# Mamba stage: the last token tile of states one to ten scaled by B on VectorE instead of GpSimd

## The chip, the cores and the metric

One core of one Trainium2 chip runs a whole two-layer decoder as one program. The metric is the device time of one execution in microseconds. The kernel before took 4200.27 us (median of 3 runs, 4198.12 to 4200.87).

Engine names: PE is TensorE (PEld its weight loads), DVE is VectorE, ACT is ScalarE, POOL is GpSimd, SP is SyncE, which issues the DMAs.

## The reference, cut to what matters

The decoder has six sublayers, each followed by a residual and a layer norm. The change lies in the fourth, a Mamba block over 32 sequences of 256 tokens, with 512 inner channels and 16 states:

```
dt    = softplus(log_dt @ W_dt.T + b_dt)          # tokens x 512
A_bar = exp(dt[..., None] * A)                    # tokens x 512 x 16
Bu    = dt[..., None] * B_coef[:, :, None, :] * xc[..., None]
h     = A_bar * h + Bu                            # along the tokens, per channel and state
y     = sum over the 16 states of h * C_coef
```

For one state s this means: u = dt * xc (tokens x 512 channels) is multiplied by one number per token, B[:, s]; a recurrence runs along the tokens for each channel; its result is multiplied by C[:, s] and summed over the states.

## The kernel before

The stage works on 16 groups of two sequences (512 tokens). Inside a group it goes through the 16 states s, and inside a state through 4 chunks c of 128 channels. I write (s, c) for such a step, and the names below are functions inside `mamba`.

For each state the work is:

- `scale_b` (L2003 on, ACT) multiplies u by B[:, s]. u lies with tokens on the partitions, in 4 token tiles of 128 x 512 (`uT`), so that B is one number per partition (`b_t`). In states 1 to 10 ACT does only three of the four tiles, and `scale_tile` on POOL (L2125, operation on L2130) does the fourth. The product is `bu`, double buffered by state.
- `turn_state` (PE, L1825) turns chunk c of `bu` with four 128x128 transposes into one of two PSUM buffers `pbu`. For c = 0 it waits for ACT's tiles and for the fourth (`tile_ready`). It also waits for the scan two steps before, whose PSUM buffer it takes.
- `decay` (ACT, L2021) makes exp(dt * A).
- `scan` (DVE, L2227) runs the recurrence on chunk c: data from `a` in SBUF and `pbu` in PSUM, result `h`.
- `times_c` (POOL, L2123) multiplies `h` by C, both read from SBUF, into `ch`.
- `sum_state` (PE, L1834) adds the turned chunk to the output `py` in PSUM, five steps later.

Between these steps each engine does, at fixed places written out by hand, the work that prepares the next group and finishes the one before. All engines work through their lists in order. Those that matter here:

- DVE: `gate` (L2235) around (0, 3) and (1, 0); `convolve` (L2197) in states 2 to 5, one operation between scans 0 and 1, two between scans 1 and 2; `finish` (L2255) before scans (7, 0), (7, 1), (10, 2), (10, 3), which waits for `rstd_of` on POOL (L2145, L2146); `one_plus` (L2207, 128x1024 f32 from SBUF to SBUF) right before scans (9, 1) and (10, 1); `lost_part` (L2213) and `take_lost` (L2221), which read two SBUF tensors each.
- PE: `project_x` (L1764) after (1, 3) to (4, 3), from the second on waiting for the convolution before; `add_skip` (L1841), `parameters` (L1787) and `spread_l` (L1794) in states 6 and 7; `project_out` (L1870, L1872) in states 4, 5, 8 and 9.
- POOL: `scale_tile(s + 1)` directly behind `times_c(s, 0)`, for s = 0 to 9; `rstd_of` behind (6, 2) and (10, 0).

Group 0 has no group before it, the last group prepares none. The groups in between run in a hardware loop whose body holds two groups.

Of the kernel before, what the change touches and what calls it, by code (L numbers as in the profile page):

```python
# [10 lines left out]
ALU = mybir.AluOpType  # L11
# [3 lines left out]
P = 128  # L15
# [1562 lines left out]
def mamba(nc, x_in, x_out, ct_dram, g_d, win_d, wout_d, conv_d, wx_d, dtp_d, alog_d, ident_d):  # L1578
# [5 lines left out]
    DI = wout_d.shape[0]  # L1584
    IC = DI // P
# [3 lines left out]
    TT = GB * T  # L1589
    GS = GB * S  # L1590
    K = N * IC
    xf_in = x_in.rearrange("(g b) (t p) d -> g p (b t) d", b=GB, p=P)
    xf_out = x_out.rearrange("(g b) (t p) d -> g p (b t) d", b=GB, p=P)
    with Stage(nc, "ma") as st:
# [28 lines left out]
        b_t = sb("b_t", [P, 2, TT, N])  # L1623
# [4 lines left out]
        uT = sb("uT", [P, 2, TT, DI])  # L1628
# [36 lines left out]
                 (wx_cols[:, :, :], wx_d.rearrange("(c p) f -> p c f", p=P)),  # L1665
                 (conv[:, :, :], conv_d), (dtp[:, :, :], dtp_d), (A[:, :, :], alog_d)]

        def on_pool(s):
            return 1 <= s <= 10

        def groups(eng, group, link=None, turns=NG // 2 - 1):
# [73 lines left out]
        def _(pe):  # L1745
# [71 lines left out]
            def turn_state(g, s, c):  # L1817

                if c == 0:
                    pe.wait_ge(bu_ready, N * g + (s + 1))  # L1820
                    if on_pool(s):
                        pe.wait_ge(tile_ready, 10 * g + s)
                pe.wait_ge(scanned, K * g + (IC * s + c + 7))
                for t in range(TT):
                    last = pe.transpose(pbu[c % 2][:, t * P:(t + 1) * P], bu[:, s % 2, t, c * P:(c + 1) * P], ident[:, :])  # L1825
                last.then_inc(bu_turned, 1)
# [110 lines left out]
        def _(act):  # L1937
# [67 lines left out]
            def scale_b(g, par, s):  # L2005

                if s == 0:
                    act.wait_ge(uT_copied, IC * g + IC)
                    act.wait_ge(b_copied, g + 1)
                act.wait_ge(bu_turned, K * g + (IC * s + 4))  # L2010
                for t in range(TT - 1 if on_pool(s) else TT):
                    last = act.activation(bu[:, s % 2, t, :], uT[:, par, t, :], ACT.Copy, scale=b_t[:, par, t, s:s + 1])  # L2012
                last.then_inc(bu_ready, 1)

# [87 lines left out]
        @block.gpsimd  # L2102
        def _(pool):
            link = Chain(pool, pool_chain, 2 * (2 + IC + 2))

            def rms_of(n):
                pool.wait_ge(ssq_ready, TT * n + TT)
                link(pool.tensor_tensor(ms[:, :], ssq[:, :], eps6[:, :], ALU.add))
                link.mark(pool.tensor_tensor(rms[:, :], ms[:, :], minus_half[:, :], ALU.pow))

            def rms_diagonal(n):
                link.wait()
                if not (type(n) is int and n == 0):
                    pool.wait_ge(xT_made, 2 * n)
                pool.tensor_tensor(rdiag[:, :, :], ident[:, :].unsqueeze(1).broadcast_to([P, TT, P]),
                                   rms[:, :].unsqueeze(2).broadcast_to([P, TT, P]), ALU.mult).then_inc(rdiag_ready, 1)

            def times_c(g, s, c):
                pool.wait_ge(scanned, K * g + (IC * s + c + 9))
                if c == 0:  # L2120
                    pool.wait_ge(c_loaded[s % 4], (4 * 16) * g + 16 * (s // 4 + 1))
                pool.wait_ge(summed, K * g + (IC * s + c + 1))
                pool.tensor_tensor(ch[:, s % 2, c], h[:, c], crep[:, s % 4, :], ALU.mult).then_inc(multiplied, 1)  # L2123

            def scale_tile(g, par, s):  # L2125

                if s == 1:
                    pool.wait_ge(uT_copied, IC * g + IC)
                pool.wait_ge(bu_turned, K * g + (IC * s + 4))
                pool.tensor_tensor(bu[:, s % 2, TT - 1, :], uT[:, par, TT - 1, :],  # L2130
                                   b_t[:, par, TT - 1, s:s + 1].broadcast_to([P, DI]), ALU.mult).then_inc(tile_ready, 1)

            def step_input(n, par, c, k):

                if k == 0:
                    pool.wait_ge(rest_ready, IC * n + (c + 1))
                    link(pool.tensor_tensor(dt[:, par, c, :], dt[:, par, c, :], ln1[:, c, :], ALU.add))
                    pool.sem_inc(dt_ready, 1)
                else:
                    pool.tensor_tensor(u[:, c, :], dt[:, par, c, :], xc[:, par, c, :], ALU.mult).then_inc(u_ready, 1)  # L2140

            def rstd_of(g, half):
                k = slice(2 * half, 2 * half + 2)
                pool.wait_ge(var_ready, 2 * g + (half + 1))
                link(pool.tensor_tensor(veps[:, k], mv[:, k, 1], eps5[:, k], ALU.add))  # L2145
                pool.tensor_tensor(rstd[:, k], veps[:, k], minus_half[:, k], ALU.pow).then_inc(rstd_ready, 1)  # L2146

            def group(g, par, first, last):
                n, prep = g + 1, not last
                ahead = not (type(g) is int and g + 2 >= NG)  # L2150
                for s in range(N):
                    for c in range(IC):
                        times_c(g, s, c)
                        if c == 0 and on_pool(s + 1):
                            scale_tile(g, par, s + 1)
                        if prep and (s, c) in ((11, 1), (12, 0), (12, 3), (13, 2)):
                            step_input(n, 1 - par, (4 * s + c - 44) // 3, 0)
                        if prep and (s, c) in ((11, 2), (12, 1), (13, 0), (13, 3)):
                            step_input(n, 1 - par, (4 * s + c - 45) // 3, 1)
                        if (s, c) in ((6, 2), (10, 0)) and not first:  # L2160
                            rstd_of(g - 1, 0 if s == 6 else 1)
                        if s == 5 and c == 2 and ahead:
                            rms_of(g + 2)
                        if s == 7 and c == 2 and ahead:
                            rms_diagonal(g + 2)

            pool.memset(eps6[:, :], 1e-6 * D)
            pool.memset(eps5[:, :], LN_EPS)
            pool.memset(ones[:, :], 1.0)
            link(pool.memset(minus_half[:, :], -0.5))  # L2170
            pool.wait_ge(w_loaded, 16 * len(loads))
            pool.sem_inc(multiplied, IC)
            pool.sem_inc(summed, 2 * IC)
            rms_of(0)
            rms_diagonal(0)
            for c in range(IC):
                for k in range(2):
                    step_input(0, 0, c, k)
            rms_of(1)
            rms_diagonal(1)  # L2180
            groups(pool, group, link, turns=NG // 2 - 2)
            for half in range(2):
                rstd_of(NG - 1, half)

        @block.vector
        def _(dve):
# [36 lines left out]
            def scan(g, s, c):  # L2223
# [3 lines left out]
                dve.tensor_tensor_scan(out=h[:, c, :], data0=a[:, s % 2, c, :], data1=pbu[c % 2][:, :],  # L2227
                                       initial=0.0, op0=ALU.mult, op1=ALU.add).then_inc(scanned, 1)

            def gate(g, par, t):  # L2230

                if t == 0:
                    dve.wait_ge(sz_ready, g + 1)
                    dve.wait_ge(summed, K * g + (K + 8))
                dve.tensor_tensor(gT[:, t, :], py[:, t, :], sz[:, par, t, :], ALU.mult).then_inc(gated, 1)  # L2235
# [24 lines left out]
            def group(g, par, first, last):  # L2260
                n, prep, ahead = g + 1, not last, not (type(g) is int and g + 2 >= NG)
                for s in range(N):
                    for c in range(IC):
                        if not first and (s, c) in ((0, 3), (1, 0)):
                            for t in (2 * s, 2 * s + 1):
                                gate(g - 1, 1 - par, t)
                        if 2 <= s < 2 + IC and c in (1, 2) and prep:
                            for k in ((1,), (2, 3))[c - 1]:
                                convolve(n, 1 - par, s - 2, k)
                        if not first and (s, c) in ((6, 0), (6, 1), (9, 2), (9, 3)):  # L2270
                            y_stats(g - 1, c)
                        if not first and (s, c) in ((6, 2), (10, 0)):
                            y_var(g - 1, 0 if s == 6 else 1)
                        if not first and (s, c) in ((7, 0), (7, 1), (10, 2), (10, 3)):
                            finish(g - 1, c)
                        if prep and (s, c) in ((9, 1), (10, 1)):
                            one_plus(n, s - 9)
                        if prep and (s, c) in ((11, 0), (12, 0)):
                            lost_part(n, s - 11)
                        if prep and (s, c) in ((11, 1), (11, 3), (12, 2), (13, 0)):  # L2280
                            take_lost(n, {(11, 1): 0, (11, 3): 1, (12, 2): 2, (13, 0): 3}[s, c])
                        scan(g, s, c)

            for p in range(2):
                dve.memset(a[:, p], 0.0)
# [469 lines left out]
```

## Time and profile before

| | |
|---|---|
| median of 3 runs | 4200.27 us |
| profiled execution | 4201.03 us, its span 4199.2 us |
| Mamba stage, first to last scan | 1342 to 3246 us from the span's start |
| mean granted TensorE clock | 0.941 of full speed |
| DVE / POOL / ACT / PE busy, whole span | 3128.6 / 2717.5 / 2909.9 / 3510.9 us |

A row of a timeline gives start, duration, engine, line, operation, written and read tensors, count, and in brackets the idle time of the engine before it with what ended it. Rows of one operation that follow each other directly are merged into one with a count, and its duration is then that of all. An operation's recorded duration holds time in which it was started and held up.

### The profile page before, as it was taken

The page shows a single profiled execution, that of the slowest core. Times are in us where ns is not written, and L with a number is a line of the kernel's source. Part 1 is how long each engine was busy: PE and PEld are TensorE (multiplying, and loading weights), DVE is VectorE, ACT ScalarE, POOL GpSimd, SP SyncE. Part 2 cuts the span into 40 slices and gives each one's busy share as a digit, 9 for nine tenths or more (in the row PEclk, how much of TensorE's full clock was granted, in tenths as well). Part 3 has the DMA queues.
Part 4 walks back from the last instruction along what each step waited for, and adds up shares of the span by engine and source line. Part 5 has one row for each costly group of instructions (what it writes and reads, how often), then busy time and mean ns, then how long its engine had stood idle before and what let it go on. Part 6 is the DMA issues. An engine that isn't in the chain of part 4 may idle for free. (4 is left out here: it accounts for less than half of the span.)

```text
span 4199.2 us, 73811 instructions
## 1 busy us (share of the span) xinstructions
PE 3510.9 (84%) x22848; PEld 2545.8 (61%) x22848; DVE 3128.6 (75%) x5241; ACT 2909.9 (69%) x5201; POOL 2717.5 (65%) x2890
## 2 busy tenths in 40 slices
PE   8996999989844888888888888888888799994666
PEld 5664666775422667666666666666667577762333
DVE  5666888844684788778878787787777477776988
ACT  2224888833565888887878888787887377774766
POOL 1224666610483998898989889898988355552555
PEclk9998999979867999999999999999999899997999
DMA  2111111151121111111111111111111111112111
GB/s 60 55 53 45 42 42 43 39 111 36 28 71 50 45 48 53 45 52 49 52 50 47 52 43 54 51 50 50 47 47 43 41 41 40 40 34 70 50 46 35
DMA packets 199386, 204.57 MB, mean 49 GB/s; under 512 B 45768, under 2 KB 164104, under 8 KB 199064
## 3 DMA queue, kind: packets, MB, share of 16 engines
q1 hardware_dynamic: 199064, 200.65, 16.3%
q8 instruction: 156, 2.56, 0.2%
q14 instruction: 166, 1.36, 0.1%
HBM read 149.18 MB, written 51.41 MB: 48 GB/s over the span
## 5 line engine op out<-in xcount | busy, mean ns | idle before, releaser
L2227 DVE TENSOR_TENSOR_SCAN ma_h<-ma_a,ma_pbu 128x512 f32<-128x512 f32 x1024 | 1223.2, 1211 | 344.9 <-PE ma_pbu L1825 180.2
L2123 POOL TENSOR_TENSOR ma_ch<-ma_h,ma_crep 128x512 f32<-128x512 f32 x1024 | 1338.1, 1324 | 201.3 <-DVE ma_h L2227 185.0
L1825 PE MATMUL ma_pbu<-ma_ident,ma_bu 128*128 128x128 f32 x4096 | 659.4, 285 | 175.9 <-DVE ma_h L2227 129.6
L1825 PEld LDWEIGHTS ma_pbu<-ma_ident,ma_bu 128*128 128x128 f32 x4096 | 484.5, 145 | 420.6 <-DVE ma_h L2227 279.6
L1834 PE MATMUL ma_py<-ma_ident,ma_ch 128*128 128x128 f32 x4096 | 637.9, 280 | 42.2 <-POOL ma_ch L2123 30.3
L2021 ACT ACTIVATE ma_a<-ma_dt,ma_A 128x510 f32<-128x510 f32 x1024 | 652.9, 717 | 1.4 <-issue 1.4
L2012 ACT ACTIVATE ma_bu<-ma_uT,ma_b_t 128x512 f32<-128x512 f32 x864 | 556.7, 718 | 11.8 <-PE ma_pbu L1825 10.1
L1834 PEld LDWEIGHTS ma_py<-ma_ident,ma_ch 128*128 128x128 f32 x4096 | 492.0, 145 | 70.2 <-POOL ma_ch L2123 64.4
L856 POOL TENSOR_TENSOR xa_prob<-xa_e,xa_rec_head 128x616 f32<-128x616 f32 x256 | 307.3, 1217 | 310.7 <-DVE xa_rec_head L945 309.9
L936 DVE TENSOR_REDUCE xa_top<-xa_pS 128x8 f32<-128x616 f32 x256 | 202.9, 793 | 149.6 <-PE xa_pS L625 142.2
L765 ACT ACTIVATE xa_eT<-xa_pE 77x512 f32<-77x512 f32 x512 | 276.7, 594 | 49.3 <-PE xa_pE L637 47.5
L637 PE MATMUL xa_pE<-xa_ident,xa_prob 128*77 128x128 f32 x2048 | 277.0, 279 | 4.8 <-POOL xa_prob L856 4.5
L637 PEld LDWEIGHTS xa_pE<-xa_ident,xa_prob 128*77 128x77 f32 x2048 | 228.2, 149 | 60.1 <-issue 32.9
L944 DVE TENSOR_REDUCE xa_esum<-xa_e 128x8 f32<-128x616 f32 x256 | 198.7, 776 | 18.3 <-ACT xa_e L760 18.1
L937 DVE TENSOR_TENSOR xa_low<-xa_pS,xa_top 128x616 f32<-128x616 f32 x256 | 204.6, 799 | 8.8
L760 ACT ACTIVATE xa_e<-xa_low 128x616 f32<-128x616 f32 x256 | 184.3, 720 | 16.8 <-DVE xa_low L937 12.0
L625 PE MATMUL xa_pS<-xa_kheads,xa_qT 64*128 64x308 f32 x1024 | 188.7, 444 | 1.6 <-issue 1.0
L337 POOL TENSOR_TENSOR la_veps<-la_mv,la_eps 128x2 f32<-128x2 f32 x32 | 6.3, 197 | 250.0 <-DVE la_mv L370 250.0
L2130 POOL TENSOR_TENSOR ma_bu<-ma_uT,ma_b_t 128x512 f32<-128x512 f32 x160 | 168.0, 1050 | 0.0
L2197 DVE SCALAR_TENSOR_TENSOR ma_xc<-ma_pm,ma_conv,ma_xc 128x510 f32<-128x510 f32 (+2 forms) x192 | 140.3, 731 | 23.2 <-ACT ma_xc L1957 20.8
L1515 POOL MEMSET scatter_eps<- 128x4 f32 x1 | 0.1, 102 | 240.5 <-POOLq L40 240.5
L1872 PE MATMUL ma_pm<-ma_wout,ma_yv 128*128 128x256 f32 x512 | 144.5, 410 | 0.0
(312 smaller groups left out, 7312.0 us busy)
## 6 DMA issues: line engine op xcount, KB each, us to landing
ma_crep<-ma_ct_dram SPq DMA_DIRECT2D x256, 256.0 KB, 3.2
xa_x<-act SPq DMA_DIRECT2D x64, 256.0 KB, 2.6
act<-xa_y SPq DMA_DIRECT2D x64, 256.0 KB, 2.2
la_x<-in_x SPq DMA_DIRECT2D x32, 256.0 KB, 2.6
act<-la_y SPq DMA_DIRECT2D x32, 256.0 KB, 2.2
ea_x<-act SPq DMA_DIRECT2D x32, 256.0 KB, 11.9
act<-ea_x SPq DMA_DIRECT2D x32, 256.0 KB, 4.0
ma_x<-act SPq DMA_DIRECT2D x16, 512.0 KB, 4.5
```

Of the source, the lines that this page charges most:

```text
L637: last = pe.transpose(pE[h][:, i, :], prob[:, u % 2, at:at + CTX], ident[:, :])
L765: act.activation(eT[:, u // T, h * HB:(h + 1) * HB, u % T, :], pE[h][:, :, :], ACT.Copy).then_inc(eT_copied, 1)
L856: pool.tensor_tensor(prob[:, u % 2].rearrange("p (h s) -> p h s", h=HC), e[:, u % 2].rearrange("p (h s) -> p h s", h=HC), rec_head[:, u, : ...
L936: link(dve.tensor_reduce(m, s, AX.X, ALU.max))
L937: dve.tensor_tensor(low[:, u % 2].rearrange("p (g h s) -> p g h s", g=2, h=HB), s, m.unsqueeze(3).broadcast_to([P, 2, HB, CTX]), ALU.subtr ...
L944: link(dve.tensor_reduce(esum[:, u % 2, :], e[:, u % 2].rearrange("p (h s) -> p h s", h=HC), AX.X, ALU.add))
L1825: last = pe.transpose(pbu[c % 2][:, t * P:(t + 1) * P], bu[:, s % 2, t, c * P:(c + 1) * P], ident[:, :])
L1834: last = pe.matmul(py[:, t, c * P:(c + 1) * P], ch[:, s % 2, c, t * P:(t + 1) * P], ident[:, :], start=(s == 0 and c == 0), stop=(s == N - ...
L2012: last = act.activation(bu[:, s % 2, t, :], uT[:, par, t, :], ACT.Copy, scale=b_t[:, par, t, s:s + 1])
L2021: act.activation(a[:, s % 2, c, :].rearrange("p (b t) -> p b t", b=GB)[:, :, 1:S], dt[:, par, c, :].rearrange("p (b t) -> p b t", b=GB)[:, ...
L2123: pool.tensor_tensor(ch[:, s % 2, c], h[:, c], crep[:, s % 4, :], ALU.mult).then_inc(multiplied, 1)
L2227: dve.tensor_tensor_scan(out=h[:, c, :], data0=a[:, s % 2, c, :], data1=pbu[c % 2][:, :], initial=0.0, op0=ALU.mult, op1=ALU.add).then_inc ...
```

## The change

`scale_tile` moves from POOL's list to DVE's. On POOL it was a product of two tensors (B broadcast along the row) behind `times_c(s, 0)`; on DVE it is a tensor_scalar with B as a pointer scalar, behind `scan(s, 0)`. On DVE it also waits for `b_copied` where s is 1. The rest (the semaphore `tile_ready`, who waits for it, ACT's three tiles) stays; `on_pool` is renamed `on_dve`.

```
-            def scale_tile(g, par, s):                      # POOL
-                if s == 1:
-                    pool.wait_ge(uT_copied, IC * g + IC)
-                pool.wait_ge(bu_turned, K * g + (IC * s + 4))
-                pool.tensor_tensor(bu[:, s % 2, TT - 1, :], uT[:, par, TT - 1, :],
-                                   b_t[:, par, TT - 1, s:s + 1].broadcast_to([P, DI]), ALU.mult).then_inc(tile_ready, 1)
...
                         times_c(g, s, c)
-                        if c == 0 and on_pool(s + 1):
-                            scale_tile(g, par, s + 1)
...
+            def scale_tile(g, par, s):                      # DVE
+                if s == 1:
+                    dve.wait_ge(uT_copied, IC * g + IC)
+                    dve.wait_ge(b_copied, g + 1)
+                dve.wait_ge(bu_turned, K * g + (IC * s + 4))
+                dve.tensor_scalar(bu[:, s % 2, TT - 1, :], uT[:, par, TT - 1, :], b_t[:, par, TT - 1, s:s + 1], None,
+                                  ALU.mult).then_inc(tile_ready, 1)
...
                         scan(g, s, c)
+                        if c == 0 and on_dve(s + 1):
+                            scale_tile(g, par, s + 1)
```

## Rows read from the trace of the kernel before

**Rows 1.** Page: engines; then line, engine, operation, count | busy, mean ns | idle.

```profile
PE 3510.9 (84%) x22848; PEld 2545.8 (61%) x22848; DVE 3128.6 (75%) x5241; ACT 2909.9 (69%) x5201; POOL 2717.5 (65%) x2890
...
L2227 DVE TENSOR_TENSOR_SCAN ma_h<-ma_a,ma_pbu 128x512 f32<-128x512 f32 x1024 | 1223.2, 1211 | 344.9 <-PE ma_pbu L1825 180.2
...
L2130 POOL TENSOR_TENSOR ma_bu<-ma_uT,ma_b_t 128x512 f32<-128x512 f32 x160 | 168.0, 1050 | 0.0
```

**Rows 2.** Busy time by stretch, two whole groups: us, then PE, PEld, DVE, ACT, POOL.

```profile
2040.66:2159.06 118.40, 103.65 (x680) 80.85 (x679) 96.22 (x103) 101.30 (x163) 107.39 (x90) 0.97 0.17 51
2159.06:2283.02 123.96, 103.44 (x681) 81.01 (x680) 96.31 (x103) 101.46 (x163) 107.56 (x90) 0.96 0.16 49
```

**Rows 3.** Groups of instructions elsewhere: DVE tensor_scalar, SBUF to SBUF.

```profile
L398 DVE TENSOR_SCALAR la_rk<-la_kv_in 128x512 f32<-128x512 f32 x32 | 13.6, 426 | 1.1
...
L2644 DVE TENSOR_SCALAR ff_wgu_f<-ff_wgu_f,ff_wscale 128x2048 f32<-128x2048 f32 x2 | 2.5, 1283 | 0.0
...
L2647 DVE TENSOR_SCALAR ff_wgu_f<-ff_wgu_f 128x2048 f32<-128x2048 f32 x2 | 2.4, 1223 | 0.0
```

**Rows 4.** Timeline of DVE, states 1 to 4 of the group from 2057.

```profile
2066.72 4.54 DVE L2227 TENSOR_TENSOR_SCAN ma_h<-ma_a,ma_pbu 128x512 f32<-128x512 f32 x4
2072.38 1.22 DVE L2227 TENSOR_TENSOR_SCAN ma_h<-ma_a,ma_pbu 128x512 f32<-128x512 f32 x1 [1.12 <-PE ma_pbu L1825]
2073.52 0.72 DVE L2197 SCALAR_TENSOR_TENSOR ma_xc<-ma_pm,ma_conv,ma_xc 128x510 f32<-128x510 f32 x1
...
2079.30 1.22 DVE L2227 TENSOR_TENSOR_SCAN ma_h<-ma_a,ma_pbu 128x512 f32<-128x512 f32 x1 [0.28 <-PE ma_pbu L1825]
...
2088.39 1.22 DVE L2227 TENSOR_TENSOR_SCAN ma_h<-ma_a,ma_pbu 128x512 f32<-128x512 f32 x1 [0.31 <-PE ma_pbu L1825]
```

**Rows 5.** Timeline of PE, end of state 2, then states 6 and 7.

```profile
2076.84 1.98 PE L1764 MATMUL ma_pm<-ma_xnT,ma_win 128*128 128x512 f32 x4 [0.32 <-DVE ma_xc L2197]
...
2099.58 0.66 PE L1825 MATMUL ma_pbu<-ma_ident,ma_bu 128*128 128x128 f32 x4 [0.81 <-DVE ma_h L2227]
...
2113.19 0.66 PE L1825 MATMUL ma_pbu<-ma_ident,ma_bu 128*128 128x128 f32 x4
```

**Rows 6.** Timeline around (0, 0): POOL; DVE; DVE in the next group.

```profile
2055.93 7.45 POOL L2123 TENSOR_TENSOR ma_ch<-ma_h,ma_crep 128x512 f32<-128x512 f32 x6
...
2062.10 1.22 DVE L2227 TENSOR_TENSOR_SCAN ma_h<-ma_a,ma_pbu 128x512 f32<-128x512 f32 x1 [1.07 <-PE ma_pbu L1825]
...
2184.74 1.22 DVE L2227 TENSOR_TENSOR_SCAN ma_h<-ma_a,ma_pbu 128x512 f32<-128x512 f32 x1 [1.34 <-PE ma_pbu L1825]
```

**Rows 7.** Timeline of DVE, states 7 and 8.

```profile
2109.16 0.54 DVE L2255 TENSOR_SCALAR ma_y<-ma_pm,ma_mv,ma_rstd 128x256 f32<-128x256 f32 x1 [2.13 <-POOL ma_rstd L2146]
...
2121.97 1.22 DVE L2227 TENSOR_TENSOR_SCAN ma_h<-ma_a,ma_pbu 128x512 f32<-128x512 f32 x1 [2.52 <-PE ma_pbu L1825]
```

**Rows 8.** Timeline of DVE, then POOL, states 9 and 10.

```profile
2127.68 0.67 DVE L2207 TENSOR_SCALAR ma_one_av<-ma_av 128x1024 f32<-128x1024 f32 x1
2128.28 1.22 DVE L2227 TENSOR_TENSOR_SCAN ma_h<-ma_a,ma_pbu 128x512 f32<-128x512 f32 x1
...
2133.57 1.17 DVE L2207 TENSOR_SCALAR ma_one_av<-ma_av 128x1024 f32<-128x1024 f32 x1
...
2136.93 0.54 DVE L2255 TENSOR_SCALAR ma_y<-ma_pm,ma_mv,ma_rstd 128x256 f32<-128x256 f32 x1 [1.06 <-POOL ma_rstd L2146]
...
2127.84 1.64 POOL L2123 TENSOR_TENSOR ma_ch<-ma_h,ma_crep 128x512 f32<-128x512 f32 x1 [0.89 <-DVE ma_h L2227]
```

**Rows 9.** Timeline ahead of group 0: DVE, then POOL.

```profile
1323.42 1.29 DVE L2221 TENSOR_TENSOR ma_gT<-ma_gT,ma_one_av 128x512 f32<-128x512 f32 x2
1324.63 2.28 DVE L2213 SCALAR_TENSOR_TENSOR ma_one_av<-ma_one_av,ma_av 128x1024 f32<-128x1024 f32 x1
...
1324.19 1.64 POOL L2137 TENSOR_TENSOR ma_dt<-ma_dt,ma_gT 128x512 f32<-128x512 f32 x1 [47.85 <-DVE ma_gT L2221]
```

**Rows 10.** Waits in the last group: total us, times, longest.

```profile
PE ma_pbu L1825 <- POOL ma_bu L2130: 4.4, 5, 1.4
```

More of the change, by code:

```diff
@@ L1666, in mamba, with on_dve @@
                  (conv[:, :, :], conv_d), (dtp[:, :, :], dtp_d), (A[:, :, :], alog_d)]
-        def on_pool(s):
+        def on_dve(s):
             return 1 <= s <= 10
@@ L1820, in turn_state @@
                     pe.wait_ge(bu_ready, N * g + (s + 1))
-                    if on_pool(s):
+                    if on_dve(s):
                         pe.wait_ge(tile_ready, 10 * g + s)
@@ L2010, in scale_b @@
                 act.wait_ge(bu_turned, K * g + (IC * s + 4))
-                for t in range(TT - 1 if on_pool(s) else TT):
+                for t in range(TT - 1 if on_dve(s) else TT):
                     last = act.activation(bu[:, s % 2, t, :], uT[:, par, t, :], ACT.Copy, scale=b_t[:, par, t, s:s + 1])
```

## The prediction

> **What bounds the kernel now.** The page's engine line first: no engine fills the span [rows 1]. The change lies in one stage, so the busy times of whole groups come next. The middle groups take 118.4 or 124.0 us by turns; the longer ones hold a 5 us gap at the loop's end. In a 118.40 us group POOL is busy 107.39, PE 103.65, ACT 101.30 and DVE 96.22 [rows 2]. By these shares POOL is the engine to relieve. The timelines say otherwise: the limit changes from state to state, and of DVE's 344.9 us of idle time ahead of scans, PE released 180.2 [rows 1]. I walked one middle group (its (0, 0) at about 2058.6) with all four engines side by side, and laid the change on it.
>
> **What leaves POOL.** 160 products of 1.05 us, 168.0 us in all, 10.5 per group [rows 1]. What that is worth depends on where POOL sets the end.
>
> **What one tile costs DVE.** The nearest row is la_rk, a tensor_scalar of the same size without a pointer scalar, 0.426 us. A pointer scalar adds 0.060 (1.283 against 1.223 at 2048 columns) [rows 3], so about 0.48. One DVE operation begins some 0.08 before the recorded end of the last: 0.67 long, 0.60 to the next start [rows 8]. So DVE's list grows by 0.40 us per tile. Bounds: 0.34 without the pointer's cost, 0.64 if it ran like the convolution, which is 0.72 long [rows 4]. I take 0.40: la_rk is the nearest row, while the convolution reads PSUM.
>
> The Trainium skill, "VectorE: DVE Perf Modes", section on the TRN2 errata, gives 58 cycles plus half the columns for this mode, 0.33 us at 0.96 GHz, an estimate; la_rk's 0.426 [rows 3] disagrees, and the row decides. By the page the 42 tiles exposed in full below would cost some 6 us less.
>
> **Where the tile is exposed, state by state.** It stands behind scan (s, 0), s = 0 to 9.
> - s = 1, 2, 3: full 0.40 each. In state 2 the list runs scan (2, 0), convolution, scan, convolution without a gap, and PE's `project_x` waits for that convolution (0.32 idle) [rows 5]; the turn of (3, 0) and scan (3, 0) wait for PE in turn (0.28) [rows 4]. State 3 repeats this. In state 1 four scans follow each other directly, PE's turn of (1, 3) needs scan (1, 1), and scan (2, 0) waits 1.12 for what PE does behind it [rows 4]. So 1.20 per group.
> - s = 4, 5: scan (4, 1) waits 0.31 for PE anyway [rows 4], (5, 1) likewise. Exposed 0.09 each, 0.18.
> - s = 6, 7: nothing. From the turn of (6, 0) at 2099.58 to that of (7, 3) at 2113.19 PE works without a wait [rows 5]. The 2.13 us that DVE waits at `finish` (7, 0) [rows 7] lies inside: POOL, a product earlier, ends this wait some 0.7 us sooner, and the tile takes 0.40 of it, but the end is PE's. No gain, no loss. If that cover were gone, 0.80 more per group.
> - s = 8: nothing; scan (8, 2) has 2.52 idle before it [rows 7].
> - s = 0: POOL is behind and runs six products in a row, 2055.93 to 2063.4, so one begins every 1.24, at 2059.65 for instance [rows 6]. DVE reaches the tile at about 2059.7 and has to let that product end (on this below). Scan (0, 1) then starts at 61.3 instead of 59.8; 1.07 of it is covered by the wait of scan (0, 2) [rows 6]. Exposed 0.35. In groups behind the loop's gap POOL is not behind and DVE has 1.34 idle [rows 6]: nothing. 8 groups x 0.35 = 2.8.
> - s = 9: the expensive one. DVE and POOL exclude each other here. `one_plus` behind scan (10, 0) is 1.17 long against 0.67 behind (9, 0), as POOL was in a product; where DVE came first, POOL's product shows 1.64 instead of 1.28 [rows 8]. Who is next? Ahead of group 0 two `take_lost` run from 1323.42 to 1324.71; POOL arrives at 1324.19; DVE's next is ready at 1324.63, and takes 2.28 where it needs 1.2, while POOL ends at 1325.83 [rows 9]. So a waiting POOL gets in between two DVE operations. In the new list the tile stands right ahead of `one_plus`. `times_c(9, 0)` becomes ready 0.16 after the tile's start [rows 8], waits for it, gets in, and `one_plus` waits 1.26. Scan (9, 1) starts 1.6 late. POOL then comes to `rstd_of` later: `times_c(10, 0)` waits for scan (10, 0), 1.6 late, and for `one_plus`; POOL had 0.5 us of backlog at that point that is now gone. DVE passes `finish` (10, 2), where it waited 1.06 [rows 8], some 1.1 us later than before. Twelve middle groups have this pattern (`one_plus` 0.67, then 1.17): 13.2 us.
>
> **States 11 to 15** keep their lists; a shift passes through.
>
> **The first and the last group.** In the last one, with nothing to prepare, POOL does set the pace, and PE waits for the POOL tile 4.4 us in all [rows 10]. Part comes back as DVE's 0.40 per state and PE's own work in states 4 and 5: I take 3 us of gain. The first group has no gates and a POOL-released wait of 0.37 in some states, about what the tile adds: +1 us, bounds 0 and 3.
>
> **The sum.** 14 middle groups x 1.38 = 19.3; + 2.8 + 13.2 + 1 - 3 = +33.3. The profiled execution took 4201.03 us (span 4199.2, 1.8 around it), 0.8 above the median. 4201.0 + 33.3 = 4234.3; I say 4234.
>
> **The rivals.**
> (a) *DVE keeps the port at s = 9*: the next DVE operation begins before the last has ended, and may follow on ahead of POOL. Only 0.4 is added there and the wait for rstd hides it. 13 less: 4221. Against it stand the rows of group 0; they are a single place.
> (b) *Tiles wait for POOL in states 1 to 3 as well.* The forecast has POOL back in step by (1, 0), so that each tile finds it between products: `times_c(2, 3)` ends within 0.05 of the place where the tile of state 3 is ready, which is close. If POOL stays one product behind, each waits half of 1.28 on average, 14 x 3 x 0.6 = 25: 4259. The Trainium skill, "SBUF — State Buffer", section Who interferes with whom, would have the one that issues second fully blocked whenever the two meet; that rule gives this rival its mechanism, and [rows 8] agree (1.64 against 1.28). It decides if POOL's lag at (1, 0) exceeds 0.7 us.
> (c) *Faster: the relieved POOL.* Place: DVE's `finish` behind `rstd_of`. POOL has 168 us less to do, and both waits, 2.13 and 1.06 [rows 7, 8], end up to 1.04 earlier. If DVE's wait at (7, 0) and not PE set the end of states 6 and 7, and PE's waits hid the tiles elsewhere, 14 groups gain 1.0 and the last one 3: 4184. It decides when PE shows idle time released by DVE between (6, 0) and (7, 3). [rows 5] show none; POOL's share of 107.39 in 118.40 speaks for it.
> (d) *The two cancel*: exposed tiles cost 1.4 per group, (c) gives back 1.0, POOL doesn't get in at s = 9: 4200 +- 8.
>
> **How the numbers follow.** Forecast 0.47, (a) 0.18, (b) 0.15, (c) 0.12, (d) 0.08. Slower by over 0.2% (8.4 us, about what can be told from no change) are the first three, 0.80; (c) gives 0.11 faster; 0.09 within. Forecast's own range: by the price of a tile, 42 x (-0.06 to +0.24) = -3 to +10, and the small terms +-3, so 4228 to 4247. The range takes in (a) and (b): 4205 to 4262; outside lie (c), half of (d) and a little above.
>
> **What would show each step.** `ma_bu` on DVE x160 at a mean of 0.5 to 0.9 us, shortest near 0.48; if the shortest is 0.65 or more, the price is wrong. DVE busy about 110 us up, POOL about 130 down (168 less, some 40 back as held-up time). `one_plus` behind (9, 0) at about 1.9 us instead of 0.67: if it stays at 0.67, (a). Waits of PE for `ma_bu` in the last group gone. Middle groups 2.2 to 2.9 us longer than 118.4 and 124.0, growth before state 4 and at state 9. The wait at (7, 0) shorter without shortening its group. Wrong altogether if states 1 to 3 keep their 7 us each.

## The result, and the profile after

The changed kernel takes 4228.9 us (median of 4 runs, 4224.87 to 4231.89), the one before 4200.35 in the same comparison (4 runs, 4198.12 to 4200.87): slower by a factor of 1.0068, interval 1.0051 to 1.0086. Its profiled execution took 4231.89 us with a span of 4230.1, 30.9 above the one before; the forecast for that difference was +33.3.

The page, the same lines as [rows 1], and then the group of the moved operation:

```profile
PE 3511.6 (83%) x22816; PEld 2556.1 (60%) x22848; DVE 3201.7 (76%) x5401; ACT 2908.9 (69%) x5201; POOL 2576.9 (61%) x2730
...
L2217 DVE TENSOR_TENSOR_SCAN ma_h<-ma_a,ma_pbu 128x512 f32<-128x512 f32 x1024 | 1224.5, 1209 | 321.3 <-PE ma_pbu L1825 163.7
```

```profile
L2226 DVE TENSOR_SCALAR ma_bu<-ma_uT,ma_b_t x160: 453/461/1586, 1343.7 to 3237.6; 128x512 f32<-128x512 f32 x160
```

The 160 tiles stand on DVE at a median of 461 ns. DVE is busy 73.1 us more, POOL 140.6 less. The busiest engine of the stage got lighter by 140 us, and the kernel got longer by 30.

Where the time appears is seen by whole groups. In the changed kernel, from gate to gate, a group that holds the loop's gap and the next one (columns as in [rows 2]):

```profile
2078.18:2203.71 125.53, 104.52 (x685) 82.83 (x684) 100.24 (x114) 101.39 (x162) 100.05 (x81) 0.96 0.17 51
2203.71:2323.92 120.21, 103.34 (x677) 80.71 (x676) 101.20 (x113) 101.28 (x162) 97.40 (x78) 0.97 0.15 47
```

The same two groups before took 123.96 and 118.33:

```profile
2063.24:2187.20 123.96, 105.11 (x684) 82.95 (x683) 96.22 (x103) 101.38 (x162) 109.59 (x92) 0.94 0.17 51
2187.20:2305.53 118.33, 101.91 (x677) 78.82 (x676) 96.24 (x103) 101.29 (x162) 105.29 (x88) 0.99 0.16 48
```

+1.57 and +1.88. Inside a group I compare when DVE reaches the same operation, counted from the group's first gate (my subtraction of starts in the two timelines; the operations are layer-norm statistics `bn`, `finish`, a scan, and the next group's gate):

| reached by DVE | before | after | shift | next group: shift |
|---|---|---|---|---|
| bn (6, 0), behind states 1 to 5 | 37.31 | 38.50 | +1.19 | +2.30 |
| scan (9, 0) | 63.30 | 62.82 | -0.48 | +0.80 |
| finish (10, 2) | 73.69 | 74.20 | +0.51 | +1.81 |
| next group's first gate | 123.96 | 125.53 | +1.57 | +1.88 |

So there are two losses where the forecast had put them (states 1 to 3: +1.19; from scan (9, 0) to finish (10, 2): +0.99 and +1.01), a gain of 1.67 and 1.50 in state 8 that it had not, and two more losses, 1.1 in state 1 of the second group and 1.06 behind the loop's gap, between the first group's finish (10, 2) and the next gate.

**States 1 and 2**, timeline of DVE (to be held against [rows 4]):

```profile
2082.79 0.46 DVE L2226 TENSOR_SCALAR ma_bu<-ma_uT,ma_b_t 128x512 f32<-128x512 f32 x1
2083.17 3.43 DVE L2217 TENSOR_TENSOR_SCAN ma_h<-ma_a,ma_pbu 128x512 f32<-128x512 f32 x3
2087.71 1.22 DVE L2217 TENSOR_TENSOR_SCAN ma_h<-ma_a,ma_pbu 128x512 f32<-128x512 f32 x1 [1.12 <-PE ma_pbu L1825]
2088.85 0.46 DVE L2226 TENSOR_SCALAR ma_bu<-ma_uT,ma_b_t 128x512 f32<-128x512 f32 x1
2089.23 0.74 DVE L2187 SCALAR_TENSOR_TENSOR ma_xc<-ma_pm,ma_conv,ma_xc 128x510 f32<-128x510 f32 x1
```

The wait of 1.12 at scan (2, 0) is the same to the hundredth: PE simply does its part later. The tile is 0.46 long and the next operation begins 0.38 after its start, and every one of these 0.38 shows at the end of the state.

**State 9**, timeline of DVE, then of POOL (against [rows 8]):

```profile
2142.14 0.46 DVE L2226 TENSOR_SCALAR ma_bu<-ma_uT,ma_b_t 128x512 f32<-128x512 f32 x1
2142.93 1.36 DVE L2197 TENSOR_SCALAR ma_one_av<-ma_av 128x1024 f32<-128x1024 f32 x1 [0.33 <-ACT ma_av L1989]
...
2149.50 0.70 DVE L2197 TENSOR_SCALAR ma_one_av<-ma_av 128x1024 f32<-128x1024 f32 x1
2151.02 1.22 DVE L2217 TENSOR_TENSOR_SCAN ma_h<-ma_a,ma_pbu 128x512 f32<-128x512 f32 x1 [0.82 <-PE ma_pbu L1825]
2152.38 0.54 DVE L2254 TENSOR_SCALAR ma_y<-ma_pm,ma_mv,ma_rstd 128x256 f32<-128x256 f32 x1
```

```profile
2142.30 1.44 POOL L2123 TENSOR_TENSOR ma_ch<-ma_h,ma_crep 128x512 f32<-128x512 f32 x1 [0.88 <-DVE ma_h L2217]
```

POOL's product is issued at 2142.30 inside the tile, is held up until the tile ends (2142.60), and ends at 2143.74. `one_plus` is issued at 2142.93 inside that product, and takes 1.36 in place of 0.67. The second `one_plus` has lost its long form (1.17). The idle time of 1.06 ahead of finish (10, 2) now lies one step earlier, as a wait of 0.82 for PE at scan (10, 1), with 0.14 left at the finish. What releases the finish is the same in both kernels: POOL's `rstd_of` ends 0.12 before it, at 2136.81 before and at 2152.26 after.

**State 8**, busy time by stretch, first two stretches of before, then of after, each beginning with PE's work behind its wait for ACT's `b_t` (2.45 us long in both kernels):

```profile
2119.00:2121.00 2.00, 2.00 (x7) 1.55 (x8) 0.45 (x1) 2.00 (x4) 2.00 (x3) 0.69 0.79 246
2121.00:2123.50 2.50, 2.50 (x12) 2.38 (x11) 1.22 (x1) 2.50 (x5) 1.28 (x2) 0.57 0.13 38
```

```profile
2135.00:2137.00 2.00, 1.95 (x12) 1.74 (x12) 0.98 (x1) 2.00 (x5) 1.92 (x2) 1.00 0.55 192
2137.00:2142.00 5.00, 5.00 (x35) 4.57 (x34) 3.44 (x3) 5.00 (x9) 2.91 (x3) 1.00 0.00 2
```

The column behind POOL is the granted clock: 0.69 and 0.57 before, so part of the stretch is at the lower level of 1.2 GHz, and 1.00 after, the level of 2.4 GHz. The rows of PE itself, before:

```profile
2118.92 0.70 PE L1870 MATMUL ma_pm<-ma_xr,ma_twice 128*128 128x256 f32 x2 [2.45 <-ACT ma_b_t L1974]
2119.45 1.62 PE L1872 MATMUL ma_pm<-ma_wout,ma_yv 128*128 128x256 f32 x4
2120.87 1.06 PE L1825 MATMUL ma_pbu<-ma_ident,ma_bu 128*128 128x128 f32 x4
```

and after:

```profile
2135.05 0.70 PE L1870 MATMUL ma_pm<-ma_xr,ma_twice 128*128 128x256 f32 x2 [2.45 <-ACT ma_b_t L1974]
2135.59 1.03 PE L1872 MATMUL ma_pm<-ma_wout,ma_yv 128*128 128x256 f32 x4
2136.45 0.60 PE L1825 MATMUL ma_pbu<-ma_ident,ma_bu 128*128 128x128 f32 x4
```

From this first matmul to the second turn behind it PE needs 3.14 us at the higher level and 4.5 to 4.8 with the lower one in it. Before, 12 of the 14 middle groups are of the long kind, after, 4 of 14. In state 1 of the second group it is the other way round; 4.8 us behind the gate, before and then after:

```profile
2192.00:2194.50 2.50, 2.48 (x18) 2.01 (x19) 2.50 (x3) 1.69 (x3) 2.45 (x3) 1.00 0.69 215
```

```profile
2208.50:2211.00 2.50, 2.50 (x13) 2.21 (x14) 2.50 (x3) 1.70 (x3) 2.29 (x2) 0.57 0.72 194
```

Behind the loop's gap the same eight matmuls of PE, before and then after, show the third place:

```profile
2184.50 1.09 PE L1834 MATMUL ma_py<-ma_ident,ma_ch 128*128 128x128 f32 x8
```

```profile
2200.09 1.91 PE L1834 MATMUL ma_py<-ma_ident,ma_ch 128*128 128x128 f32 x8
```

The granted clock there is 0.90 from 2184 to 2187 before and 0.74 from 2200.5 to 2203.5 after.

### The profile page after: what moved, and what is told of

It is laid out like the page before. It is cut to its first block and busy times, and to the rows that moved or that the text cites. A ratio compares the mean times of both kernels' runs of the same rounds, so it can differ in the third digit from the quotient of the medians.

```text
span 4230.1 us, 73779 instructions
## 1 busy us (share of the span) xinstructions
PE 3511.6 (83%) x22816; PEld 2556.1 (60%) x22848; DVE 3201.7 (76%) x5401; ACT 2908.9 (69%) x5201; POOL 2576.9 (61%) x2730
## 5 line engine op out<-in xcount | busy, mean ns | idle before, releaser
L2123 POOL TENSOR_TENSOR ma_ch<-ma_h,ma_crep 128x512 f32<-128x512 f32 x1024 | 1354.8, 1337 | 369.4 <-DVE ma_h L2217 349.0
L651 PE MATMUL xa_pG<-xa_eT,xa_v 77*32 77x256 f32 x2048 | 139.6, 385 | 1.6 <-ACT xa_eT L765 1.6
L661 PE MATMUL xa_pG<-xa_wo,xa_oT 128*128 128x256 f32 x512 | 139.5, 396 | 1.0 <-ACT xa_oT L770 1.0
```

## The experiments

Runs named together shared one chip and the runs of the kernel before; ratios are to these. "Shift" is counted as in the table above.

**Three parts of the change** (before: 4201.09), and the tile taken away altogether. In `tiles_2_3_4` only the tiles of states 2 to 4 go to DVE, in `tiles_7_8_9` and `tile_10` those named; the others stay on POOL, with a semaphore of their own:

```
-        def on_pool(s):
-            return 1 <= s <= 10
+        DVE_TILES, POOL_TILES = (2, 3, 4), (1, 5, 6, 7, 8, 9, 10)
+        def on_dve(s):  return s in DVE_TILES
+        def on_pool(s): return s in POOL_TILES
```

> Only the tiles of states 2, 3 and 4, those behind scans (1, 0), (2, 0) and (3, 0), move to DVE; the other seven stay on POOL. Theory, exposure by place: 0.39 us for each of these three in 14 middle groups, 16.4 us, so about 4217. Rival, every tile costs alike (28.5 us over 160 tiles, 0.18 each): 48 tiles make 8.6, so 4209. Rival, POOL's relief counts: below 4200.

4223.89 us, 1.0056 (1.0042 to 1.007), +22.8. Shift at bn (6, 0): +1.24 in the group that holds the gap, as in the full change. Three tiles make most of the loss. More than their 14 x 1.2 = 17 came out, and more than the 4217 that I expected. In this kernel, too, state 8 became short in most groups (10 of 14), and yet the group kept +0.87 at bn (9, 2), since `one_plus` (9, 0) then waits 0.71 for ACT's exponential and meets POOL.

> Only the tiles of states 7, 8 and 9, behind scans (6, 0), (7, 0) and (8, 0), move to DVE. Theory, exposure by place: PE sets the end there, so 4200 within 4, less a little (up to 3) for the last group. Rival, every tile costs alike: 4209. Rival, POOL's relief counts, as the wait at finish (7, 0) gets shorter: down to 4190.

4201.11 us, 1.0002 (0.9993 to 1.0011): nothing. DVE at finish (7, 0), against [rows 7], then at scan (8, 2):

```profile
2108.62 0.54 DVE L2273 TENSOR_SCALAR ma_y<-ma_pm,ma_mv,ma_rstd 128x256 f32<-128x256 f32 x1 [1.32 <-POOL ma_rstd L2155]
...
2122.08 1.22 DVE L2236 TENSOR_TENSOR_SCAN ma_h<-ma_a,ma_pbu 128x512 f32<-128x512 f32 x1 [1.97 <-PE ma_pbu L1833]
```

The wait for POOL went from 2.13 to 1.32, so POOL is relieved as counted, and bn (9, 2) comes at 66.18 as before. That fits PE setting the end of these states.

> Only the tile of state 10, behind scan (9, 0) and right ahead of one_plus, moves to DVE. Theory, POOL gets in between the two: one_plus behind (9, 0) grows from 0.67 to 1.9 us, and the wait at finish (10, 2) can hide only part: +7 to +13, so 4207 to 4213. Rival, DVE keeps the port and one_plus stays at 0.67: 4200 within 3. Rival, every tile costs alike: 4203.

4220.29 us, 1.0042 (1.0029 to 1.0056), +19.2, above the 7 to 13 that I expected: one tile per group costs nearly as much as three in states 2 to 4. DVE, then POOL, in state 9:

```profile
2135.55 0.46 DVE L2245 TENSOR_SCALAR ma_bu<-ma_uT,ma_b_t 128x512 f32<-128x512 f32 x1
2135.93 1.77 DVE L2216 TENSOR_SCALAR ma_one_av<-ma_av 128x1024 f32<-128x1024 f32 x1
```

```profile
2135.72 1.44 POOL L2131 TENSOR_TENSOR ma_ch<-ma_h,ma_crep 128x512 f32<-128x512 f32 x1 [0.89 <-DVE ma_h L2236]
```

`one_plus` is issued at 2135.93, right at the tile's end, and POOL has been waiting since 2135.72. POOL's product ends at 2137.16, `one_plus` at 2137.70: it ran behind it. Shift at finish (10, 2): +1.03 and +1.19. Over the 14 middle groups that is 12.4 us, within my 7 to 13. In a group with the gap another 1.2 follows behind the gap (7.6 us in all), and that is what I had not counted.

> Leaves out part of the computation: the fourth token tile of states 1 to 10 is multiplied by B nowhere; POOL has 160 products less and DVE none more. Theory, POOL is not the limit of the middle groups: only the last group gains, 3 us, so 4197, with up to 5 either way from stretches at the lower TensorE clock. Rival, POOL's relief counts in each group (1 to 2 us from the waits for rstd): 4170 to 4185.

Here the last token tile of states 1 to 10 is multiplied by nothing and holds zeros. 4197.64 us, 0.9989 (0.998 to 0.9998), -3.5. In the profile the last group shrinks from 93.6 to 90.7 us, and the 14 middle ones keep their length (0.4 us less in all). The first group grows by 2.7, of which 1.7 lie in state 6 with the granted clock at 0.61 where it was 1.00, and what lies ahead of the stage is 3.4 shorter, which no tile touches. So POOL's relief is worth 3 us, in the last group; that the whole kernel shows about the same number is partly chance.

**The places of the change** (before: 4199.75). `tile_10_later` puts the tile of state 10 behind scan (9, 1); `behind_scan_2` those of states 2 to 5 behind scans (1, 2) to (4, 2):

```
-                        if c == 0 and on_dve(s + 1):
+                        if c == (1 if s == 9 else 0) and on_dve(s + 1):         # tile_10_later
+                        if c == (2 if 1 <= s <= 4 else 0) and on_dve(s + 1):    # behind_scan_2
```

> The changed kernel, but the tile of state 10 stands behind scan (9, 1) instead of (9, 0), so not next to one_plus any more. Theory, POOL gets in between the two: one_plus behind (9, 0) returns to about 0.67, the end moves 6 to 12 us below the changed kernel, 4217 to 4223. Rival, the cost at state 9 is the tile's own 0.4 us and ACT's timing: within 3 of the changed kernel, 4226 to 4232.

4223.26 us, 1.0056 (1.0043 to 1.007), some 5 below the changed kernel by the ratios, whose intervals overlap. `one_plus` (9, 0) is 0.67 in the four middle groups whose state 8 is long and 1.20 to 1.30 in the ten whose state 8 is short: the tile no longer stands ahead of it, but where PE wins time in state 8 it meets POOL's product all the same. The middle groups are 6.7 us shorter than in the changed kernel, and only 1.8 of that lies between scan (9, 0) and finish (10, 2); the rest lies where stretches at the lower clock moved. So this run confirms what stretches `one_plus`, and does not price it; `tile_10` does.

> The changed kernel, but the tiles of states 2 to 5 stand behind scans (s, 2), after the convolutions, instead of (s, 0). All 160 tiles are still on DVE. Theory, the place counts: PE's project_x waits for the convolution, and behind (s, 2) DVE has 0.28 us of wait ahead of the next state to cover the tile, so 0.3 of 0.39 come back in states 1 to 3, 13 us and more with the 1.1 us of lower clock in state 1: 4210 to 4217. Rival, the amount of work on DVE counts: 4229 within 3.

4220.34 us, 1.0047 (1.0033 to 1.0061), some 9 below the changed kernel by the ratios (their intervals touch), and less of a gain than I expected (4210 to 4217). The shift at bn (6, 0) is +0.10 where it was +1.19, so the three states are freed. State 9 costs what it did, DVE:

```profile
2135.16 0.46 DVE L2226 TENSOR_SCALAR ma_bu<-ma_uT,ma_b_t 128x512 f32<-128x512 f32 x1
2135.54 1.78 DVE L2197 TENSOR_SCALAR ma_one_av<-ma_av 128x1024 f32<-128x1024 f32 x1
```

No wait for ACT ahead of `one_plus` now, hence the full 1.78, and a shift of +1.13 at finish (10, 2): the forecast's 1.1. What was lost again lies elsewhere. Over the 14 middle groups DVE wins 16.0 us on the changed kernel up to bn (6, 0), but 8.6 fewer are gained in states 6 to 8, as state 8 is long in 9 of 14 groups again, and 2.9 more are lost behind finish (10, 2); from scan (9, 0) to finish (10, 2) both kernels lose 12.3.

**Work added, none taken away**, same runs of the kernel before. `both` leaves POOL its ten tiles and lets DVE multiply each a second time, into a spare tensor:

```
+                dve.tensor_scalar(spare[:, :], uT[:, par, TT - 1, :], b_t[:, par, TT - 1, s:s + 1], None, ALU.mult)
...
+                        if c == 0 and on_pool(s + 1):
+                            scale_spare(g, par, s + 1)
```

> The kernel before, with POOL's tiles as they were, and ten extra tiles per group on DVE in the places of the changed kernel, written to a spare tensor nobody reads. It has the cost on DVE without the relief of POOL. Theory: as the changed kernel in states 1 to 3, worse at states 0, 9 and in the last group, where POOL is behind: 4232 to 4245. Rival, POOL's relief gave back 12 us (the three parts run alone cost 41 and not 29): 4240 or more would bear it out. Rival, tile and POOL work don't disturb each other: 4229.

4230.19 us, 1.0068 (1.0055 to 1.0082), the ratio of the changed kernel, and a little below the 4232 to 4245 that I expected; the rival's 4229 is nearer. Part of that is chance. The last group is 94.4 us (93.6 before, 91.8 in the changed kernel), worse as expected, and the first is 2.3 us longer than in the changed kernel; but the middle groups grow by 25.3 and not 29.0 us, since state 8 is short in 13 of them and not in 10. The tiles' cost up to bn (6, 0) and from scan (9, 0) to finish (10, 2) is that of the changed kernel to 0.3 us. So what the change costs in the middle groups is what DVE takes on; what POOL gets rid of is worth nothing there.

**A better version?** `best_places` (same runs) puts the tiles of states 2 to 9 on DVE, 2 to 5 behind the third scan, and leaves 1 and 10 on POOL.

> DVE takes the tiles of states 2 to 9 only, those of states 2 to 5 behind scans (s, 2); POOL keeps the tiles of states 1 and 10. Theory, no tile is exposed and the last group gains: 4196 to 4203. Rival, the amount counts (0.18 us for each of 128 tiles): 4223.

4201.87 us, 1.0005 (0.9996 to 1.0014). 128 tiles on DVE for nothing, and nothing gained.

**ACT's order in state 8** (before: 4197.85). As PE waits 2.45 us for `b_t` there, `copy_b` goes ahead of the decay on ACT: in the kernel before, in the changed one, and in `best_places`.

```
+                    if s == 8 and prep:
+                        copy_b(n, np_)
...
-                    if s == 8 and prep:
-                        copy_b(n, np_)
```

> The kernel before, with one edit on ACT: copy_b (L1974) stands ahead of decay of state 8 instead of behind it, so that PE's project_out at (8, 1) is released 2.4 us sooner and PE neither waits 2.45 us nor runs at the lower clock behind that wait. It asks what sets states 8 and 9. Theory, PE behind that wait sets them: each of 14 middle groups gets up to 2.4 us shorter, 34 us, less what DVE and the wait for rstd at finish (10, 2) take back; 4170 to 4190. Rival, states 8 and 9 are set by DVE or ACT anyway: 4200 within 4.

4196.92 us, 0.9997 (0.9988 to 1.0006): missed, I had expected 4170 to 4190. DVE, then POOL:

```profile
2121.85 1.22 DVE L2227 TENSOR_TENSOR_SCAN ma_h<-ma_a,ma_pbu 128x512 f32<-128x512 f32 x1 [2.01 <-ACT ma_a L2021]
2124.47 1.50 DVE L2207 TENSOR_SCALAR ma_one_av<-ma_av 128x1024 f32<-128x1024 f32 x1 [1.41 <-ACT ma_av L1989]
```

```profile
2124.38 1.04 POOL L2130 TENSOR_TENSOR ma_bu<-ma_uT,ma_b_t 128x512 f32<-128x512 f32 x1
```

PE no longer waits, and DVE reaches scan (9, 0) 29.1 us sooner, summed over the middle groups. By finish (10, 2) 24.5 of these are gone. ACT is what is late next: its decay (2.01) and its exponential (1.41), and `one_plus` now falls into POOL's tile. States 8 and 9 have two limits close together, PE and ACT.

> The changed kernel with the same edit on ACT. In the profile of the changed kernel the lower clock in state 8 is gone already, which hid 1.7 us in every second group. Theory: the edit is worth less here than on the kernel before if that clock was the gain, or as much if the wait was; then one_plus behind (9, 0), no longer waiting for PE's states, shows POOL getting in between at its full price. 4200 to 4220, a difference to the kernel before with the same edit of 28 to 38 us.

4205.66 us, 1.0017 (1.0008 to 1.0026). This is 8.7 above `early_b_before`, where I had expected 28 to 38: missed. Of the 0.68% that the changed kernel had lost only a quarter is left. DVE, then POOL:

```profile
2130.57 0.46 DVE L2226 TENSOR_SCALAR ma_bu<-ma_uT,ma_b_t 128x512 f32<-128x512 f32 x1
2132.06 0.69 DVE L2197 TENSOR_SCALAR ma_one_av<-ma_av 128x1024 f32<-128x1024 f32 x1 [1.03 <-ACT ma_av L1989]
```

```profile
2130.73 1.43 POOL L2123 TENSOR_TENSOR ma_ch<-ma_h,ma_crep 128x512 f32<-128x512 f32 x1 [1.69 <-DVE ma_h L2217]
```

The tile runs inside DVE's wait for ACT, and POOL's product, though it gets in between, ends at 2132.16, 0.10 after `one_plus` is issued. The same tile behind the same scan costs nothing once DVE has to wait behind it anyway. Here POOL's relief is worth something in the middle groups, too: with its tile gone, `one_plus` takes 0.69 and not 1.50, and of the 29.1 us won at scan (9, 0) only 13.0 are lost by finish (10, 2), 11.5 fewer than in `early_b_before`. That pays for most of the 15.2 us more that the tiles cost up to bn (6, 0).

> DVE has the tiles of states 2 to 9 in covered places, POOL those of 1 and 10, and copy_b stands ahead of decay of state 8. Theory: no tile is exposed, so within 4 us of the kernel before with the edit on ACT alone, 2 or 3 less for the last group. Rival, with PE's wait gone DVE sets states 6 to 9 and the tiles there are exposed: 5 to 15 us above it.

4197.97 us, 1.0002 (0.9993 to 1.0011). No version beats the kernel before by more than can be measured.

## Why the prediction was right, step by step

The sign, the mechanism of the two large terms and the size held: +33.3 forecast, +30.9 in the profiles and +28.5 by the medians. The sum is closer than its terms were, since terms that I did not have cancel each other; that part is luck. The table has all runs, by stretches of a group: profiled us against the kernel before, the middle four columns summed over the 14 middle groups, the first group counted from its first scan to the next gate, the last from its first gate to its last.

| run | first group | to bn (6, 0) | to scan (9, 0) | to finish (10, 2) | to next gate | last group |
|---|---|---|---|---|---|---|
| the changed kernel | +3.4 | +23.1 | -12.5 | +12.3 | +6.1 | -1.8 |
| `tiles_2_3_4` | +2.6 | +20.3 | -13.0 | +6.8 | +7.3 | -3.4 |
| `tile_10` | -0.2 | +2.8 | -0.5 | +12.4 | +7.6 | -1.1 |
| `tiles_7_8_9` | +0.3 | 0.0 | -1.3 | +0.8 | +0.5 | +0.1 |
| `no_tile` | +2.7 | +2.9 | -7.4 | +1.1 | +3.0 | -2.9 |
| `tile_10_later` | +3.2 | +19.7 | -12.3 | +10.5 | +4.4 | -2.0 |
| `behind_scan_2` | 0.0 | +7.1 | -3.9 | +12.3 | +9.0 | -1.0 |
| `both` | +5.7 | +23.3 | -17.2 | +12.4 | +6.8 | +0.8 |
| `best_places` | +0.2 | +2.9 | -5.7 | +3.5 | +2.4 | -2.8 |
| `early_b_before` | +0.1 | +1.5 | -29.1 | +24.5 | +1.9 | +0.6 |
| `early_b_after` | +3.1 | +16.6 | -29.1 | +13.0 | +0.1 | -3.1 |
| `early_b_best` | +0.3 | +2.9 | -29.0 | +26.6 | +3.7 | -1.3 |

These are single profiles. What lies ahead of the stage, which no edit touches, alone differs by up to 4.5 us between them.

- **The price of a tile.** Forecast 0.48 long and 0.40 net; measured 0.46 and 0.38. The mean is 0.53 (84.4 us in 160), since nine tiles stretch to 1.5 to 1.6 where POOL is in a product. DVE's busy time grew by 73.1, where I said about 110. The estimate from the Trainium skill ("VectorE: DVE Perf Modes", section on the TRN2 errata), 0.33, is too low against these rows. The same section says so of that formula and gives some 150 cycles, measured, in place of the 58. With half the columns that makes an estimate of 0.42, which agrees with la_rk's 0.426 and is 0.04 short of the 0.46.
- **States 1, 2, 3.** 1.20 forecast, 1.19 measured, and `behind_scan_2` takes it away (+0.10). Each of these tiles is 0.46 long, so POOL was between products, against rival (b). Times 14 it is 16.7 us.
- **States 4, 5.** 0.18 forecast, nothing measured. The tiles ahead of the first convolution of states 2, 3, 4 and 5 start 0.39, 0.78, 1.19 and 1.19 later than the convolution did before (10.28 to 10.67, 17.20 to 17.98, 24.11 to 25.30, 31.49 to 32.68 from the gate): one step each for states 1, 2 and 3, and none for 4. At bn (6, 0) it is 1.19 still.
- **States 6, 7, 8.** Zero forecast, zero measured in `tiles_7_8_9`. Also right: the shorter wait for `rstd_of` (2.13 to 1.32; forecast some 0.7 less POOL, 0.81 measured) moves no end. This is where rival (c) fell, and (d) with it; `no_tile`, whose middle groups keep their length, and `both` speak against it as well.
- **State 0.** 0.35 in every second group forecast. The tile is held up as described (1.48 to 1.58 long behind (0, 0) in 8 of the 14 groups), but of the shift about 0.1 is left at the gate. Over-sized by some 2 us in all.
- **State 9.** POOL gets in between the tile and `one_plus`, against rival (a): 1.77 in `tile_10`, 1.78 in `behind_scan_2`, forecast 1.9. The Trainium skill ("SBUF — State Buffer", section Who interferes with whom) has the second to issue blocked fully. These rows agree for each pair (the product held up until the tile ends, `one_plus` until the product ends), and add who is served when POOL waits and DVE has the next one ready. From scan (9, 0) to finish (10, 2) the forecast had +1.1; measured +0.99, +1.01, and +1.13 where the clock is as before; 12.3 us over the middle groups against 13.2. The way there was partly another: in ten of the 14 groups `one_plus` is 1.36 and not 1.77, because it waits 0.33 for ACT first. These are the very ten in which state 8 is short: PE brings scan (9, 0) sooner, and ACT has become the later one.
- **First and last group.** First gate 1461.05 to 1464.61, +3.6 where I said +1 (bounds 0 to 3: above them). The waits of 0.37 that were to cover the tiles are there as before, and the tiles come on top: +2.1 by scan (6, 0), 0.4 for each of the states 1 to 5. PE's wait ahead of scan (6, 1) adds 1.3 (1.71 for 0.45), in a stretch with the clock at 0.62 where it was 1.00, and state 9 gives 0.7 back. Without tiles behind scans (1, 0) to (4, 0), in `behind_scan_2`, the first gate comes at +0.4. The last group 93.59 to 91.84, -1.75 where I said -3. `no_tile` shows the 3 us that POOL's side is worth there, and DVE's tiles take back more than I gave them.
- **The middle groups as a whole.** The 14 grow by 29.0 us (with +3.6 and -1.75 that is 30.8), where I had 35.3. Forecast 2.2 to 2.9 longer each; measured 1.2 to 2.0 in the ten from the third on (1.57 and 1.88 in those shown), 2.0 to 4.1 in the other four. A whole kind of term is absent from the prediction: it took TensorE's speed as given. State 8 gets 1.67 and 1.50 back in the two groups shown, as PE runs it at the 2.4 GHz level. Over the 14 groups the time of this piece of PE's list falls by 12.5 us (62.9 to 50.4). The lower level turns up in state 1 (+1.1 in six groups, 6.4 us) and behind the gap (+0.7 to +1.1 in each of six groups, 5.6 of the 6.1 us). So -12.5 stands against some +12, and the near agreement of 29.0 with the terms that I had (16.7 + 12.3) is luck.

For the two groups shown the table of shifts closes: +1.19 - 1.67 + 0.99 + 1.06 = +1.57 for the first group; for the second, +1.2 + 1.1 - 1.50 + 1.01 + 0.07 = +1.88, the last term being state 0 and rounding.

The parts (22.8 + 0 + 19.2) give more than the whole (28.5), and the table shows where. In the middle groups `tiles_2_3_4` and `tile_10` sum to 43.7 us against 29.0. Up to bn (6, 0) and from there to scan (9, 0) their sums are those of the whole (23.1; -13.5 against -12.5). From scan (9, 0) to finish (10, 2) they are 6.9 us more: in `tiles_2_3_4` a state 8 shorter by 1.67 leaves only 0.37 of shift less at bn (9, 2), as `one_plus` waits for ACT and meets POOL, and `tile_10` pays for meeting POOL again; in the whole it is one meeting. The other 8.8 us lie behind finish (10, 2): each part loses 7.3 and 7.6 us there, the whole only 6.1. Why the loss behind the gap does not add up is not shown.

Open stays what decides in which states the lower level falls. PE's wait of 2.45 us ahead of the piece is the same in both kernels, while the granted clock behind it is 0.69 and 1.00. I saw it move with nearly every edit and made no experiment on it. That the lower level is the cause of the piece's length is read from its rows and the granted clock, not from a run that holds the clock fixed.

## What to carry to other kernels

Price a moved operation by the place it gets, not by the engine it leaves: the same 0.38 us cost 0.4 behind one scan and 0.1 for three tiles together behind the scan two further on, and the busiest engine's relief was worth 3 us in 4200. That value, too, belongs to the schedule: with ACT's order changed the same relief took 11.5 us out of state 9. Where VectorE and GpSimd exclude each other, do not put two such VectorE operations back to back at the moment when GpSimd becomes ready; 0.46 us of work cost 1.1 there, and nothing where a wait lay between the two. And before a wait is removed, look for what is late next: behind PE's 2.45 us in state 8 stood ACT with 2.01 and 1.41.

## What the runs showed of the hardware

- In state 9, a GpSimd product that waits for a VectorE operation is served ahead of VectorE's next one, even when that follows directly: `one_plus` took 1.77 and 1.78 us instead of 0.67. The product itself is issued 0.3 us before the tile ends, and its recorded duration grows from 1.28 to 1.44.
- Stretches of TensorE at the lower clock level are part of this kernel's schedule. A piece of 3.14 us takes 4.8 with one in it (four transposes 1.06 instead of 0.60), and they move from one state to another between kernels whose other engines differ by 0.1 to 1.2 us ahead of them: in state 8, 12 of 14 groups had one before, 9 in `behind_scan_2`, 4 in the changed kernel, 1 in `both`.
- A tensor_scalar of 128x512 f32 with a pointer scalar, SBUF to SBUF, takes 0.46 us (median of 160), against 0.426 with an immediate in [rows 3].
